# A four-block graph network on one core: gate banks awaited one by one, VectorE's state update moved, expert layers without a barrier between them

## The chip, the cores and the metric

The kernel runs on one core of one Trainium2 chip. Times are device microseconds of that core, median of three runs. TensorE (PE) multiplies matrices into eight PSUM banks, VectorE (DVE) and ScalarE (ACT) work on elements, GpSimd (POOL) does next to nothing here, SyncE (SP) issues most of the transfers (ScalarE can issue some as well). Each engine works through its own list of instructions in order; between engines there are semaphores.

## The reference, cut to what matters

3125 nodes with 128 features, 100000 edges. Four blocks stand one behind the other, each behind a layer norm and with a residual: a gated graph network (GRU cell, four layers), a graph convolution, a relational convolution with eight edge types, and a mixture of eight experts in three layers. The change touches the first and the last.

```python
# gated block, four layers, weights w_ih and w_hh shared
m = x @ weight[l]
agg = segment_sum(m[src], dst)
gi = agg @ w_ih.T + b_ih
gh = x @ w_hh.T + b_hh
r = sigmoid(i_r + h_r)
z = sigmoid(i_z + h_z)
n = tanh(i_n + r * h_n)
x = (1.0 - z) * n + z * x
# expert block, three layers
agg = segment_sum(h[src], dst) / deg
logits = concatenate([h, agg]) @ router_W[l] + router_b[l]
gates = softmax(top_k(logits, 2))
weak = relu(agg @ weak_W[l] + weak_b[l])              # 4 experts
sh = relu(agg @ strong_W1[l] + strong_b1[l])          # 4 experts
strong = sh @ strong_W2[l] + strong_b2[l]
h = h + sigmoid(h @ conf_W[l] + conf_b[l]) * (gates over experts)
```

## The kernel before

**Tiles.** Nodes are cut into 25 tiles of 128 and seven chunks `CH` of 512, 512, 384, 512, 384, 512 and 309 columns, one PSUM bank each. The sum over edges is a product with the dense matrix of edge counts `A` (fp8), which stays in SBUF: per chunk and tile two matmuls (high and low half of the float16 pair), 50 in all.

**Gated block (`block_gru`, `pe_gru`, `act_gru`, `dve_gru`).** Four layers l = 0 to 3, chunks ci = 0 to 6 in each. TensorE: `sum_tile` (L972) sums over edges; `gate_b` (L949) makes the products with the old state into banks BR, BZ and BH; `gate_c` (L959) adds those of the sums and fills BI. ScalarE: sigmoids into `g_r` and `g_z` (L1052, L1054), tanh into `g_n` (L1056). VectorE's `gate_c`: gate sum (L1143, L1146), then after the tanh the state update (L1148, L1151, L1153) into `g_ht`. `finish` of a chunk: TensorE turns the new state to node order in bank 7 (L754), ScalarE writes the high half of `g_h16` or `g_h16b` (L1066) and of `ht16` (L1045), VectorE the low halves (L1167, L1134). Before `gate_b` of chunk n TensorE waits until all banks of chunk n-1 are read out, in three waits together.

Among all this the block does work for a later one, the *mirror steps* (`class Symmetric`): blocks of packed counts are turned by TensorE into bank 6 or 7 in turn (L851), and VectorE adds them to `sym_blocks` (L870). A mirror step of TensorE waits until the step before the last has been added, and in bank 7 also until the last `finish` has freed it (L1167).

The order is written out by hand. In layer 0 the sums of all but two chunks exist before the block begins, and for each chunk ci = 1 to 6 TensorE does `gate_b(ci)`, some sums of layer 1, a mirror step, `gate_c(ci)`, the turning of chunk ci-1, a mirror step. VectorE does a mirror addition, the whole of `gate_c(ci)`, `finish(ci-1)`, a mirror addition. In layers 1 to 3 the gates of chunk ci run among the 25 tiles of the sums of chunk ci+1, by the table `AMONG`: `a` (sums to float16), `b`, `c` (the gates) and `S` (a mirror step) stand before the tile of that number; VectorE and TensorE follow the same table. The last chunk's gates run outside the table.

**Expert block (`block_experts`).** An input stage (layer norm, first product, per-layer scales of the weights) ends in a barrier of all engines. `sp_inputs` stores x to `x_parked`. Then each of three layers runs `dve_layer`, `act_layer`, `pe_layer` and `sp_layer`, and a barrier stands behind each. At a layer's start VectorE finds the largest |h| (L1845 in the first, L1847 in the others), with TensorE's help for the maximum over partitions, and from it a scale (last instruction L1856). ScalarE issues seven transfers for the layer (L2019 to L2025: router and confidence weights and biases, strong bias 1, the two bias rows `m_bias`) and then writes the high halves of `h16` (L2028), VectorE the low halves (L1861), TensorE sums over the edges (L2125). SyncE loads ten weight pieces, each into a room of `wroom`; ScalarE (L2035) and VectorE (L1879) split piece k from room k+1 into a pair in room k, four of them before the first chunk's work, six among it. Then it loads `invd` for each chunk (L1838). L2200 are the weak experts' products, L2164 and L2183 the strong ones'.

## Time and profile before

| | |
|---|---|
| median of three runs (lowest, highest) | 3316.8 us (3315.81, 3319.97) |
| profiled execution, time and span | 3323.0 us, 3320.6 us |
| busy: TensorE, VectorE, ScalarE | 2987.0, 2182.6, 895.6 us |
| mean granted TensorE clock | 0.959 of full |
| gated block | 350 to 822 us |
| expert block, input stage | 1651 to 1696 us |
| expert layers | 1696 to 2228, 2228 to 2757, 2757 to 3287 us |

Times in rows are microseconds from the span's start, where "ns" doesn't stand beside them. In a timeline, the bracket at the end is how long the engine sat idle before the row, and what ended that; rows that repeat directly are merged ("x8"), and the second number is then the time of all. "issue" means that nothing that the profile shows was waited for; ACTq and SPq are transfers issued by ScalarE and SyncE. A granted clock of 1.00 is 2.4 GHz, 0.50 is 1.2 GHz, the only two levels. A buffer's name without its number stands for all of its kind.

### The profile page before, as it was taken

What the parts mean: (1) busy time and instruction counts of PE and PEld (TensorE: products, weight loads), DVE (VectorE), ACT (ScalarE), POOL (GpSimd) and SP (SyncE); (2) the same over time, 40 slices, a digit from 0 to 9 for tenths busy, and PEclk for the clock granted to TensorE, in tenths of its full rate; (3) what the DMA queues carried; (4) which work ended last, traced back from release to release, by engine and by line L of the source; (5) the groups of instructions that cost most, each with busy time, mean ns of one, the idle gap of its engine ahead of it and who ended that gap; (6) DMA issues with size and microseconds to landing.
All of it is one profiled execution on the core that took longest, in us unless ns stands there. A gap on an engine that the chain in (4) does not pass through costs nothing. (4 is left out here: it accounts for less than half of the span.)

```text
span 3320.6 us, 47504 instructions
## 1 busy us (share of the span) xinstructions
PE 2987.0 (90%) x18761; PEld 1792.3 (54%) x18761; DVE 2182.6 (66%) x3982; ACT 895.6 (27%) x1667; POOL 16.7 (1%) x22
## 2 busy tenths in 40 slices
PE   3888789998897999999869999979999997999997
PEld 2666445555443444444535656655666564566565
DVE  7999445555227766766667656676667585666676
ACT  3888322111101000000023222223222233222222
POOL 1000000000000000000000000000000000000000
PEclk8899899999998999999979999999999998999999
DMA  5455246766005555544220000011000002000001
GB/s 123 141 150 157 80 154 220 227 210 201 1 1 164 160 168 165 175 143 135 82 83 3 4 3 4 3 45 40 3 6 5 3 1 83 3 4 3 4 3 41
DMA packets 310958, 265.84 MB, mean 80 GB/s; under 512 B 32767, under 2 KB 289409, under 8 KB 308174
## 3 DMA queue, kind: packets, MB, share of 16 engines
q1 hardware_dynamic: 295694, 256.14, 25.2%
q10 hardware_dynamic: 14624, 5.76, 0.7%
q8 instruction: 153, 2.51, 0.3%
q0 software_dynamic: 416, 0.85, 0.1%
q14 instruction: 71, 0.58, 0.1%
HBM read 172.67 MB, written 90.05 MB: 79 GB/s over the span
## 5 line engine op out<-in xcount | busy, mean ns | idle before, releaser
L1544 PE MATMUL psum<-r_wd,r_h 128*128 128x512 fp8e4 (+1 forms) x2600 | 567.8, 374 | 13.4 <-ACT r_h L226 12.7
L2164 PE MATMUL psum<-m_agg,m_weights 128*128 128x512 f16 (+2 forms) x2016 | 429.5, 366 | 26.9 <-ACT m_agg L2071 26.8
L2125 PE MATMUL psum<-counts,m_h 128*128 128x512 fp8e4 (+2 forms) x2100 | 417.2, 355 | 29.5 <-DVE m_h L1861 29.5
L2183 PE MATMUL psum<-m_weights,x_nodes 128*128 128x256 f16 (+1 forms) x3600 | 413.0, 273 | 17.7 <-DVE m_wtmp L1969 15.6
L1544 PEld LDWEIGHTS psum<-r_wd,r_h 128*128 128x128 f16 x2600 | 240.0, 96 | 306.0 <-issue 16.5
L2183 PEld LDWEIGHTS psum<-m_weights,x_nodes 128*128 128x128 f16 (+1 forms) x3600 | 350.4, 98 | 75.1 <-DVE m_wtmp L1969 22.4
L2125 PEld LDWEIGHTS psum<-counts,m_h 128*128 128x128 f16 x2100 | 206.6, 98 | 226.8 <-issue 37.8
L2164 PEld LDWEIGHTS psum<-m_agg,m_weights 128*128 128x128 f16 x2016 | 198.8, 102 | 240.7 <-issue 56.3
L2083 ACT ACTIVATE m_hT<-m_hT,m_g 128x256 f32<-128x256 f32 x300 | 135.5, 500 | 599.5 <-DVE m_hT L1983 599.5
L2071 ACT ACTIVATE m_agg<-psum,x_nodes 128x512 f32<-128x512 f32 (+2 forms) x336 | 236.4, 716 | 144.4 <-PE psum L2164 116.5
L1983 DVE SCALAR_TENSOR_TENSOR m_hT<-psum,x_nodes,m_bias 128x512 f32<-128x512 f32 (+1 forms) x150 | 112.0, 750 | 169.9 <-PE psum L2200 169.9
L1969 DVE SCALAR_TENSOR_TENSOR m_wtmp<-psum,x_nodes,m_bias 128x256 f32<-128x256 f32 (+1 forms) x300 | 144.8, 483 | 119.9 <-PE psum L2183 116.4
L1960 DVE TENSOR_TENSOR x_nodes<-m_agg,x_nodes 128x512 f16<-128x512 f32 (+2 forms) x336 | 209.7, 624 | 11.6
L2200 PE MATMUL psum<-m_weights,m_agg 128*128 128x512 f16 x900 | 206.5, 379 | 0.0
L676 PE MATMUL psum<-oh_c,oh_s 128*128 128x150 f16 x1566 | 156.2, 237 | 48.5 <-ACT counts L711 31.4
L870 DVE TENSOR_TENSOR sym_blocks<-sym_blocks,psum 128x1024 uint16<-128x1024 uint16 (+1 forms) x169 | 110.4, 664 | 118.6 <-PE psum L851 118.0
L1559 ACT ACTIVATE r_ags<-psum 128x512 f32<-128x512 f32 (+1 forms) x52 | 26.9, 569 | 581.3 <-PE psum L1544 581.3
L676 PEld LDWEIGHTS psum<-oh_c,oh_s 128*128 128x128 f16 x1566 | 112.2, 100 | 111.2 <-issue 68.1
L710 ACT ACTIVATE strip<-psum 128x600 uint16<-128x600 f32 x239 | 162.4, 680 | 34.6 <-PE psum L676 32.8
L972 PE MATMUL psum<-counts,g_h16b 128*128 128x512 fp8e4 (+2 forms) x700 | 159.7, 359 | 2.7 <-DVE g_h16b L1167 2.7
L1972 DVE SCALAR_TENSOR_TENSOR m_h<-m_wtmp,m_g,m_h 128x256 f32<-128x256 f32 (+1 forms) x300 | 145.3, 484 | 10.7
L1276 PE MATMUL psum<-counts,g_h 128*128 128x512 fp8e4 (+2 forms) x700 | 137.2, 355 | 15.9 <-ACT g_h L226 15.2
(290 smaller groups left out, 3389.1 us busy)
## 6 DMA issues: line engine op xcount, KB each, us to landing
r_wd<-packed_sym SPq DMA_DIRECT2D x120, 640.0 KB, 4.2
packed_counts<-strip SPq DMA_DIRECT2D x21, 1800.0 KB, 7.8
sym_blocks<-packed_counts SPq DMA_DIRECT2D x88, 384.0 KB, 4.7
packed_sym<-sym_blocks SPq DMA_DIRECT2D x84, 384.0 KB, 3.3
w_stage<-in_L_gnn_strong_W SPq DMA_DIRECT2D x12, 1024.0 KB, 6.4
m_weights<-in_L_gnn_strong_W SPq DMA_DIRECT2D x21, 512.0 KB, 9.0
x_parked<-x_nodes SPq DMA_DIRECT2D x2, 1600.0 KB, 5.7
x_nodes<-x_parked SPq DMA_DIRECT2D x2, 1600.0 KB, 6.2
```

The source lines that it names most:

```text
L676: m = pe.matmul(psum[:, unit_at(u, w):unit_at(u, w) + UC], oh_s[q][:, k, :, v], oh_c[q][:, k, :, v], start=True, stop=True)
L710: act.activation(typed_home, typed, ACT.Copy, scale=0.5).then_inc(kept_a, 1)
L972: m = pe.matmul(bank[bk][:, 0:cw], h16[l % 2][:, part, i, :], A[:, i, c_:c_ + cw], start=(i == 0 and part == 0), stop=(i == NT - 1 and par ...
L1544: m = pe.matmul(bank[pair[b]][:, 0:2 * cw], h16[:, part, p0 + i, :], f_[:, 2 * b:2 * b + 2, :], start=(p0 + i == 0 and part == 0), stop=(p ...
L1960: vec.tensor_tensor(s_[:, BANK:BANK + cw], wide32, s_[:, 0:cw], ALU.subtract).then_inc(s_split, 1)
L1969: vec.scalar_tensor_tensor(tmp[k % 2][0:r_, :], bank[6 + k % 2][0:r_, 0:H], k_strong[0:r_], bcast[0:r_, ge * H:(ge + 1) * H], ALU.mult, AL ...
L1972: vec.scalar_tensor_tensor(h2[0:r_, i, :], tmp[k % 2][0:r_, :], gates[ci % 2][0:r_, k, ge:ge + 1], h2[0:r_, i, :], ALU.mult, ALU.add).then ...
L2071: act.activation(agg[:, hh % 2, 0:cw], bank[4 + hh % 2][:, 0:cw], ACT.Relu, bias=b1s[:, e * FB + f:e * FB + f + 1], scale=k_hidden).then_i ...
L2125: m = pe.matmul(bank[kb][:, 0:cw], h16[:, part, i, kb * P:(kb + 1) * P], A[:, i, c_:c_ + cw], start=(i == 0 and part == 0), stop=(i == NT ...
L2164: m = pe.matmul(bank[4 + hh % 2][:, 0:cw], w_[:, i, kb, f * P:(f + 1) * P], agg16[:, j, kb, 0:cw], start=(x_ == 0), stop=(x_ == len(todo) ...
L2183: m = pe.matmul(bank[b_][0:r_, 0:H], s_[:, pa[0] * BANK + k * P:pa[0] * BANK + k * P + r_], w_[:, pa[1], f, :], start=(f == 0 and pa == PA ...
L2200: m = pe.matmul(bank[2 + pr % 2][0:r_, :], agg16[:, pa[0], kb, k * P:k * P + r_], w_[:, pa[1], kb, :], start=(y_ == 0), stop=(y_ == len(to ...
```

## The change

Three parts, all in the order of instructions and in waits; the arithmetic is the same.

1. *Gates.* TensorE waits before each group of `gate_b` for its own bank only, for BH until the gate sum's first operation has read it (`g_gated`), and the wait for BI moves to `gate_c`, ahead of its third group.
2. *State.* VectorE's `gate_c` is cut into `gated` (L1142, L1145 afterwards) and `state` (L1152, L1155, L1157). In layer 0 from chunk 1 on `finish(ci-1)` and a mirror addition stand between them; in layers 1 to 3 one mirror addition does, by the letter `d` in the table. Chunk 0 of layer 0 and the last chunk of each layer keep their order.
3. *Experts.* ScalarE issues none of the layer transfers any more. Router and confidence weights and biases of all three layers (now in tiles with room for three) and the bias rows of the first are issued by SyncE in the input stage, behind a clearing by GpSimd that VectorE did before. `sp_layer` loads the pieces of the next layer as soon as the last user of a room in the layer before is through (`room_used`), then the bias rows when the last strong product is added, then `invd`. One barrier stands behind the third layer, none between them.

```diff
@@ -886,7 +886,7 @@
-        AMONG = {1: "S", 3: "a", 4: "S", 6: "S", 7: "b", 9: "S", 11: "c", 13: "S", 16: "S", 19: "S", 22: "S"}
+        AMONG = {1: "S", 3: "a", 4: "S", 6: "S", 7: "b", 9: "S", 11: "c", 13: "Sd", 16: "S", 19: "S", 22: "S"}
...
-                    if n:
-                        pe.wait_ge(g_reset_kept, n)
-                        pe.wait_ge(g_update_kept, n)
-                        pe.wait_ge(g_gated_sum, n)
-                    for g, bk in enumerate((BR, BZ, BH)):
+                    for g, (bk, left) in enumerate(((BR, g_reset_kept), (BZ, g_update_kept), (BH, g_gated))):
+                        if n:
+                            pe.wait_ge(left, n)
...
                     for g, (bk, made_of) in enumerate(((BR, g_reset), (BZ, g_update), (BI, g_input))):
+                        if bk == BI and n:
+                            pe.wait_ge(g_gated_sum, n)
...
-                    gate_c(0, ci)
+                    gated(0, ci)
                     if ci == 0:
+                        state(0, ci)
                         gate_a(0, EARLY + 1)
-                    if ci:
+                    else:
                         finish(0, ci - 1)
                         sym.dve_step()
+                        state(0, ci)
...
+            def load_biases(l):
+                sp.dma_start(bcast[:, 0:NWK * H], bass.AP(m_wb.tensor, m_wb.offset + l * NWK * H, [[0, P], [1, NWK * H]])).then_inc(mbb_in, 16)
+                sp.dma_start(bcast[:, NWK * H:NE * H], bass.AP(m_b2.tensor, m_b2.offset + l * NSG * H, [[0, P], [1, NSG * H]])).then_inc(mbb_in, 16)
...
+                    sp.wait_ge(prio_made, 2)
+                    for l in range(NLAY):
+                        sp.dma_start(rw[:, l, :, 0:NE], m_rw[l].rearrange("(k p) e -> p k e", p=P)).then_inc(mrw_in, 16)
+                        sp.dma_start(rw[:, l, 0:KB, NE:NE + 1], m_cw[l].rearrange("(k p) e -> p k e", p=P), allow_slow_non_contiguous=True).then_inc(mrw_in, 16)
+                        sp.dma_start(rb[:, l, 0:NE], bass.AP(m_rb.tensor, m_rb.offset + l * NE, [[0, P], [1, NE]])).then_inc(mrw_in, 16)
+                        sp.dma_start(rb[:, l, NE:NE + 1], bass.AP(m_cb.tensor, m_cb.offset + l, [[0, P], [1, 1]])).then_inc(mrw_in, 16)
+                        sp.dma_start(b1[:, l], m_b1[l].rearrange("e (k p) -> p (e k)", p=P), allow_slow_non_contiguous=True).then_inc(mrw_in, 16)
+                    load_biases(0)
...
+                def room_used(l, k):
+
+                    if k + 1 == NPC:
+                        sp.wait_ge(s_mixed, NSG * NT * (l + 1))
+                        return
+                    n_, e = ORDER[k + 1]
+                    if n_ == "w1":
+                        sp.wait_ge(s_hidden, hidden_at(l, NCH - 1, e, FB - 1) + 1)
+                    elif n_ == "w2":
+                        sp.wait_ge(s_mixed, mixed_at(l, NCH - 1, e, len(tiles_of(CH[NCH - 1])) - 1) + 1)
+                    else:
+                        sp.wait_ge(k_mixed, NPR * NT * (l + 1))
...
+                        if l:
+                            room_used(l - 1, k)
...
+                    if l:
+                        sp.wait_ge(s_added, NSG * NT * l)
+                        load_biases(l)
...
                 def act_layer(l):
-                    if l == 0:
-                        act.wait_ge(steps.handle, mark["rw_cleared"])
-                    act.dma_start(rw[:, :, 0:NE], m_rw[l].rearrange("(k p) e -> p k e", p=P)).then_inc(mrw_in, 16)
...
-                    act.dma_start(bcast[:, NWK * H:NE * H], bass.AP(m_b2.tensor, m_b2.offset + l * NSG * H, [[0, P], [1, NSG * H]])).then_inc(mbb_in, 16)
                     act.wait_ge(steps.handle, mark["h_scale", l])
...
                     sp_layer(l)
-                    barrier()
+                barrier()
```

*VectorE, gated block, layer 0, chunk 1.* `g_t` is the gate sum's room, `g_h16b` the split state of chunk 0, `sym_blocks` the mirror additions. Before:

```order
L1143 SCALAR_TENSOR_TENSOR g_t_60<-psum,g_sc,g_r_56 128x512
L1146 TENSOR_TENSOR g_t_60<-g_t_60,psum 128x512
L1148 TENSOR_TENSOR g_t_60<-g_ht,g_n_62 128x512
L1151 TENSOR_TENSOR g_t_60<-g_t_60,g_z_58 128x512
L1153 TENSOR_TENSOR g_ht<-g_t_60,g_n_62 128x512
L1167 SCALAR_TENSOR_TENSOR g_h16b<-psum,g_h16b 128x512
L1134 SCALAR_TENSOR_TENSOR g_hn<-g_ht,g_hn 128x512
L870 TENSOR_TENSOR sym_blocks_47<-sym_blocks_47,psum 128x2x512
```

The same place afterwards:

```order
L1142 SCALAR_TENSOR_TENSOR g_t_60<-psum,g_sc,g_r_56 128x512
L1145 TENSOR_TENSOR g_t_60<-g_t_60,psum 128x512
L1171 SCALAR_TENSOR_TENSOR g_h16b<-psum,g_h16b 128x512
L1134 SCALAR_TENSOR_TENSOR g_hn<-g_ht,g_hn 128x512
L870 TENSOR_TENSOR sym_blocks_47<-sym_blocks_47,psum 128x2x512
L1152 TENSOR_TENSOR g_t_60<-g_ht,g_n_62 128x512
L1155 TENSOR_TENSOR g_t_60<-g_t_60,g_z_58 128x512
L1157 TENSOR_TENSOR g_ht<-g_t_60,g_n_62 128x512
```

The three state operations went from ahead of the finish and the mirror addition to behind them.

*VectorE, gated block, layer 1, gates of chunk 1 among the sums of chunk 2.* Before:

```order
L1146 TENSOR_TENSOR g_t_60<-g_t_60,psum 128x512
L1148 TENSOR_TENSOR g_t_60<-g_ht,g_n_62 128x512
L1151 TENSOR_TENSOR g_t_60<-g_t_60,g_z_58 128x512
L1153 TENSOR_TENSOR g_ht<-g_t_60,g_n_62 128x512
L870 TENSOR_TENSOR sym_blocks_49<-sym_blocks_49,psum 128x2x256
L870 TENSOR_TENSOR sym_blocks_46<-sym_blocks_46,psum 128x2x512 x3
```

and afterwards:

```order
L1145 TENSOR_TENSOR g_t_60<-g_t_60,psum 128x512
L870 TENSOR_TENSOR sym_blocks_49<-sym_blocks_49,psum 128x2x256
L1152 TENSOR_TENSOR g_t_60<-g_ht,g_n_62 128x512
L1155 TENSOR_TENSOR g_t_60<-g_t_60,g_z_58 128x512
L1157 TENSOR_TENSOR g_ht<-g_t_60,g_n_62 128x512
L870 TENSOR_TENSOR sym_blocks_46<-sym_blocks_46,psum 128x2x512 x3
```

One mirror addition, that of the step at tile 13, went ahead of the state operations.

*ScalarE, start of the first expert layer* (`m_xT` belongs to the input stage, `m_rw` to `m_bias` are the layer's transfers, `m_h` is `h16`). Before:

```order
L1719 ACTIVATE m_xT_120<-psum 128x128
L2019 DMA m_rw<-in_L_gnn_router_W 128x4x8
L2020 DMA m_rw<-in_L_gnn_conf_W 128x2x1
L2021 DMA m_rb<-in_L_gnn_router_b 128x8
L2022 DMA m_rb<-in_L_gnn_conf_b 128x1
L2023 DMA m_b_127<-in_L_gnn_strong_b 128x16x1
L2024 DMA m_bias<-in_L_gnn_weak_b 128x1024
L2025 DMA m_bias<-in_L_gnn_strong_b 128x1024
L2028 ACTIVATE m_h_125<-m_h,m_sc 128x1280 x5
```

and afterwards:

```order
L1744 ACTIVATE m_xT_121<-psum 128x128
L2059 ACTIVATE m_h_126<-m_h,m_sc 128x1280 x5
L2066 ACTIVATE m_weights<-m_weights,m_wmax_115 128x1024 x4
L2076 ACTIVATE m_hT<-psum 128x512 x2
L2085 ACTIVATE m_agg_105<-m_agg,m_sc 128x1024
```

The seven transfers are gone from this queue, in all three layers; on SyncE's they stand in the input stage, and the bias rows of layers 1 and 2 between the weight pieces and `invd`.

## Rows read from the trace of the kernel before

**Rows 1.** Busy time by stretch: us, PE, PEld, DVE, ACT, POOL, clock, DMA, GB/s.
```profile
389.00:450.80 61.80, 41.86 (x180) 22.56 (x181) 29.11 (x50) 16.47 (x29) 0.00 (x0) 0.80 0.28 91
...
462.00:578.00 116.00, 109.49 (x666) 67.75 (x663) 63.35 (x103) 23.00 (x38) 0.00 (x0) 1.00 0.69 218
```
**Rows 2.** Timeline of TensorE, gated block, layer 0: start, us, what.
```profile
389.04 1.09 PE L851 MATMUL psum<-ident,sym_blocks 128*128 128x128 f32 x4 [4.36 <-DVE g_h16b L1167]
389.92 3.09 PE L949 MATMUL psum<-g_hn,gate_w 128*128 128x384 f16 x9
...
395.33 1.63 PE L959 MATMUL psum<-x_nodes,gate_w 128*128 128x384 f16 x9
396.79 0.60 PE L754 MATMUL psum<-ident,g_ht 128*128 128x128 f32 x4
...
450.81 0.63 PE L851 MATMUL psum<-ident,sym_blocks 128*128 128x128 f32 x4 [3.48 <-DVE g_h16b L1167]
```
**Rows 3.** Timeline of ScalarE, the same layer, chunks 1 and 6.
```profile
385.30 0.81 ACT L1056 ACTIVATE g_n<-g_t,g_b,g_sc 128x512 f32<-128x512 f32 x1 [0.87 <-DVE g_t L1146]
...
386.54 0.57 ACT L1066 ACTIVATE g_h16b<-psum 128x512 f16<-128x512 f32 x1
...
448.94 0.57 ACT L1066 ACTIVATE g_h16b<-psum 128x512 f16<-128x512 f32 x1
```
**Rows 4.** Timeline of VectorE, the same layer, chunks 1 and 6.
```profile
388.21 0.68 DVE L1167 SCALAR_TENSOR_TENSOR g_h16b<-psum,g_h16b 128x512 f16<-128x512 f32 x1
...
449.98 0.68 DVE L1167 SCALAR_TENSOR_TENSOR g_h16b<-psum,g_h16b 128x512 f16<-128x512 f32 x1
```
**Rows 5.** Timeline of TensorE, layer 1, mirror steps at tiles 19 and 22.
```profile
490.24 0.63 PE L851 MATMUL psum<-ident,sym_blocks 128*128 128x128 f32 x4 [1.27 <-DVE sym_blocks L870]
...
491.68 0.60 PE L851 MATMUL psum<-ident,sym_blocks 128*128 128x128 f32 x4
```
**Rows 6.** Timeline of VectorE, the same place.
```profile
487.62 0.69 DVE L1148 TENSOR_TENSOR g_t<-g_ht,g_n 128x512 f32<-128x512 f32 x1 [0.88 <-ACT g_n L1056]
...
489.68 1.01 DVE L870 TENSOR_TENSOR sym_blocks<-sym_blocks,psum 128x512 uint16<-128x512 uint16 x2
```
**Rows 7.** Who waited for whom, 462 to 822 us (us, times, longest); a timeline row.
```profile
PE psum L851 <- DVE sym_blocks L870: 13.8, 13, 1.8
...
570.76 0.63 PE L851 MATMUL psum<-ident,sym_blocks 128*128 128x128 f32 x4 [0.46 <-DVE sym_blocks L870]
```
**Rows 8.** Timeline of ScalarE, start of expert layer 1.
```profile
2227.84 0.45 ACTq L2019 DMA_DIRECT2D m_rw<-in_L_gnn_router_W  x1
...
2230.95 6.27 ACTq L2024 DMA_DIRECT2D m_bias<-in_L_gnn_weak_b  x1
...
2237.78 6.37 ACT L2028 ACTIVATE m_h<-m_h,m_sc 128x1280 f16<-128x1280 f32 x5 [16.66 <-issue]
```
**Rows 9.** Timeline of VectorE, the same place.
```profile
2227.88 0.16 DVE L1847 TENSOR_REDUCE m_sc<-m_hmax 128x1 f32<-128x7 f32 x1 [0.39 <-PEq L104]
...
2229.97 0.15 DVE L1856 TENSOR_SCALAR m_sc<-m_sc 128x1 f32<-128x1 f32 x1
```
**Rows 10.** Timelines of VectorE, ScalarE and SyncE around expert layer 0's start.
```profile
1705.34 0.15 DVE L1856 TENSOR_SCALAR m_sc<-m_sc 128x1 f32<-128x1 f32 x1
...
1707.16 6.37 ACT L2028 ACTIVATE m_h<-m_h,m_sc 128x1280 f16<-128x1280 f32 x5 [14.83 <-issue]
...
1651.02 0.33 SPq L1705 DMA_DIRECT2D x_parked<-x_nodes  x1
1696.20 3.15 SPq L1831 DMA_DIRECT2D m_weights<-in_L_gnn_strong_W  x5
```
**Rows 11.** Timeline of TensorE, first sums of expert layer 1.
```profile
2240.94 23.02 PE L2125 MATMUL psum<-counts,m_h 128*128 128x512 fp8e4 x100 [11.83 <-DVE m_h L1861]
```
**Rows 12.** Timeline of TensorE, a weak product and what follows it.
```profile
2197.12 2.76 PE L2200 MATMUL psum<-m_weights,m_agg 128*128 128x512 f16 x12
2199.72 1.74 PE L2164 MATMUL psum<-m_agg,m_weights 128*128 128x309 f16 x12
```

More of the change, by code:

```diff
@@ L1135, in state_low, with gated @@
                                              ALU.subtract).then_inc(made, 1)
-                def gate_c(l, ci):
-                    n, q = l * NCH + ci, ci % 2
-                    c_, cw = CH[ci]
-                    h_, r_, z_, t_, n_ = ht[:, c_:c_ + cw], rr[q][:, 0:cw], zz[q][:, 0:cw], tt[q][:, 0:cw], nn[q][:, 0:cw]
+                def gated(l, ci):
+                    n, q, cw = l * NCH + ci, ci % 2, CH[ci][1]
+                    r_, t_ = rr[q][:, 0:cw], tt[q][:, 0:cw]
                     vec.wait_ge(g_reset_kept, n + 1)
@@ L1146, in gate_c, with state @@
                     vec.tensor_tensor(t_, t_, bank[BI][:, 0:cw], ALU.add).then_inc(g_gated_sum, 1)
+                def state(l, ci):
+                    n, q = l * NCH + ci, ci % 2
+                    c_, cw = CH[ci]
+                    h_, z_, t_, n_ = ht[:, c_:c_ + cw], zz[q][:, 0:cw], tt[q][:, 0:cw], nn[q][:, 0:cw]
                     vec.wait_ge(g_new, n + 1)
@@ L1183, in among @@
                             if what == "c" and gates_of is not None:
-                                gate_c(l, gates_of)
+                                gated(l, gates_of)
+                            if what == "d" and gates_of is not None:
+                                state(l, gates_of)
                 gate_a(0, EARLY)
@@ L1205, in dve_gru @@
                             gate_a(l, ci)
-                            gate_c(l, ci)
+                            gated(l, ci)
+                            state(l, ci)
                         if 0 < ci < LC:
@@ L1660, in build_program @@
     e_high, e_low = sem("e_high"), sem("e_low")
-    mrw_in, mb1_in, mbb_in, inv_in = sem("mrw_in"), sem("mb1_in"), sem("mbb_in"), sem("inv_in")
+    mrw_in, mbb_in, inv_in = sem("mrw_in"), sem("mbb_in"), sem("inv_in")
     piece_in = [sem(f"piece_in{k}") for k in range(2 * NSG + NWK // 2)]
@@ L1675, in block_experts @@
         NSH = 6
+        MRW_IN = 80 * NLAY
         NPR = NWK * H // BANK
@@ L1679, in block_experts @@
             bcast = sbuf(c, "m_bias", [P, NE * H], F32)
+            b1 = sbuf(c, "m_b1", [P, NLAY, NSG * FB], F32)
             agg = sbuf(c, "m_agg", [P, KB, BANK], F32)
@@ L1682, in block_experts @@
             hT = sbuf(c, "m_hT", [P, KB, BANK], F32)
-            rw = sbuf(c, "m_rw", [P, 2 * KB, NE + 1], F32)
-            rb = sbuf(c, "m_rb", [P, NE + 1], F32)
+            rw = sbuf(c, "m_rw", [P, NLAY, 2 * KB, NE + 1], F32)
+            rb = sbuf(c, "m_rb", [P, NLAY, NE + 1], F32)
             sc = sbuf(c, "m_sc", [P, 4], F32)
@@ L1702, in pool_inputs @@
                               allow_small_or_imprecise_dtypes=True).then_inc(prio_made, 1)
+                    pool.memset(rw[:, :, KB:2 * KB, NE:NE + 1], 0.0).then_inc(prio_made, 1)
                 def sp_inputs():
                     sp.dma_start(xpark, xn[:].rearrange("p i f -> p (i f)")).then_inc(parked, 16)
+                    sp.wait_ge(prio_made, 2)
[6 more added lines that the diff above has]
+                    load_biases(0)
                     sp.wait_ge(parked, 16)
@@ L1771, in block_experts @@
                 wroom = sbuf(c0, "m_weights", [P, NPC, SL], F32)
-                b1 = sbuf(c0, "m_b1", [P, NSG * FB], F32)
                 xroom = xn[:].rearrange("p i f -> p (i f)")
@@ L1842, in dve_layer @@
                     if l == 0:
-                        vec.memset(rw[:, KB:2 * KB, NE:NE + 1], 0.0).then_inc(steps.handle, steps.up())
-                        mark["rw_cleared"] = steps.n
                         vec.tensor_reduce(sc[:, 0:1], h2[:], axis=AX.XY, op=ALU.max, apply_absolute_value=True).then_inc(steps.handle, steps.up())
@@ L1870, in dve_layer @@
                     vec.tensor_tensor(k_weak, sc[:, 2:3], w_inv["ww"], ALU.mult).then_inc(steps.handle, steps.up())
-                    vec.tensor_scalar(b1s[:], b1[:], ks[:, 1:2], None, ALU.mult).then_inc(steps.handle, steps.up())
+                    vec.tensor_scalar(b1s[:], b1[:, l], ks[:, 1:2], None, ALU.mult).then_inc(steps.handle, steps.up())
                     settle()
@@ L1898, in route @@
                         vec.wait_ge(prio_made, 1)
-                        vec.wait_ge(mrw_in, 64 * (l + 1))
+                        vec.wait_ge(mrw_in, MRW_IN)
                         vec.wait_ge(e_routed, n + 1)
@@ L2143, in route @@
                         pe.wait_ge(h_kept, KB * (n + 1))
-                        pe.wait_ge(mrw_in, 64 * (l + 1))
+                        pe.wait_ge(mrw_in, MRW_IN)
                         for i, k in tiles_of(CH[ci]):
```

11 lines of the change are left out of this document (3 added, 8 removed).

## The prediction, made before the changed kernel had run

> **What bounds the kernel now.** I read the busy shares by stretch first, then the timeline of each engine around TensorE's pauses, then the list of who waited for whom. In the stretches that the change touches TensorE is the engine that sets the time: in layer 1 of the gated block (462 to 578 us) it is busy 109.49 of 116 us at a granted clock of 1.00, while VectorE has 63.35 us of work [rows 1]. So a change pays there only where it shortens a pause of TensorE. There are three kinds of such pauses.
>
> - Layer 0 of the gated block, chunks 1 to 6: TensorE is busy only 41.86 of 61.8 us, at a clock of 0.80 [rows 1]. Once per chunk it stops before a mirror step (L851) until VectorE has written `g_h16b` (L1167): 4.36 us in the first of six, 3.48 us in the last [rows 2].
> - Layers 1 to 3: TensorE stops before a mirror step until VectorE has added an earlier one (L870): 13 times, 13.8 us together [rows 7]. An example is 1.27 us at 490.24 [rows 5].
> - The start of each expert layer: TensorE sits idle 11.83 us before its first sums (2240.94) [rows 11], behind ScalarE, which issues seven transfers before its first conversion at 2237.78 [rows 8], though the scale that it needs is there at 2229.97 + 0.15 = 2230.12 [rows 9].
>
> **Gate banks waited for one by one.** In layers 1 to 3 and in layer 0, what frees the banks of chunk n is finished long before TensorE comes to chunk n+1: in layer 0 the pause described above ends behind the whole state update already. The split waits win nothing. Do they cost? Each chunk gets three more waiting matmuls. A row bounds it: twelve matmuls of 512 columns in two groups, each group with waits of its own that are long met, take 2.76 us with the drain, and the next instruction starts 2.60 us after the first, 217 ns each [rows 12]. So 0 us; the bounds are 0 and 27 chunks x 3 x 0.02 = 1.6 us of loss.
>
> **Layer 0: the finish of the chunk before moves ahead of the state update.** Before, VectorE's order is gate sum, (tanh on ScalarE), three state operations, then L1167. Behind the three state operations L1167 starts at 388.21 [rows 4]. Afterwards it follows the gate sum at once, but it also needs ScalarE's half of the same split (L1066), and ScalarE does that behind the tanh: L1056 at 385.30, L1066 at 386.54 for 0.57 us [rows 3]. It ends at 387.11; with 0.1 us for the hand-over L1167 can start at 387.2 instead of 388.21: 1.0 us. So not the whole state update (three operations of 0.69 us each, as in [rows 6]) is saved: ScalarE is late next. The same subtraction in the six chunks gives 1.0, 0.6, 1.2, 0.6, 1.2 and 0.4 us (the last: 449.98 less 448.94 + 0.57 + 0.1 [rows 3, 4]), together **5.0 us**. The state update itself now waits behind the mirror step and is ready about 4 us after TensorE's restart; TensorE asks for it (L754) only behind the next chunk's gates, 396.79 - 389.04 = 7.75 us after the restart [rows 2], so it is covered with 3 to 4 us to spare. Were that cover gone, each us of lateness would count six times.
>
> **Layers 1 to 3: one mirror addition between gate sum and state.** Before, the addition of the step at tile 13 stands behind the state update: VectorE ends the gate sum at 487.62 - 0.88 = 486.74, sits idle for the tanh until 487.62, updates the state, and starts the addition at 489.68 [rows 6]; TensorE was ready for its step at tile 19 at 490.24 - 1.27 = 488.97 [rows 5]. Afterwards the addition (0.42 to 0.69 us) fills the idle 0.88 us, so the pause at tile 19 goes. What is late next is the addition of tile 16's step: the state still ends at about 489.68, this addition at 490.4, and TensorE asks for it one station later, 491.68 - 490.24 = 1.44 us [rows 5] after 488.97, at 490.41. With the hand-over 0.1 us of 1.27 stays. Where the sums have 309 columns instead of 384, each station (tiles 13, 16 and 19) is 0.2 us shorter, so about 0.6 us of such a pause stays. The 13 pauses are three beside 512-column sums, six beside 384, two beside 309, and two like the one of 0.46 us at 570.76 [rows 7], which belong to the last chunk's gates, whose order doesn't change. So 13.8 - 0.9 = 12.9 us can go, and 6 x 0.1 + 2 x 0.6 = 1.8 us stay: **11.1 us** (bounds 0, if the wait only moves to tile 22, and 12.9).
>
> **Expert layers.** The seven transfers leave ScalarE's queue; ScalarE can start its conversion when the scale is there. At the start of layer 1 that is 2237.78 - 2230.12, less 0.07 of hand-over: 7.6 us [rows 8, 9]; layer 2 shows the same rows; at the start of layer 0, where VectorE's reduction of all of `h` covers most of it, 1707.16 - 1705.49 - 0.07 = 1.6 us [rows 10]. Everything behind it (halves of `h16`, sums, weight splits) runs in a chain paced by VectorE, ScalarE and TensorE, not by a transfer, and moves with it. The barrier itself: VectorE's first reduction of the layer (2227.88) comes 0.39 us after its last instruction [rows 9]; without it a hand-over of 0.04 is left: 0.35 us, twice. The weight pieces are now fetched when their rooms come free, so they are earlier than before except for the last two, which follow the last strong product and are needed some 40 us later. On SP's queue the `invd` row of the next layer stands behind these pieces and two bias transfers (one of the kind took ScalarE 6.27 us to issue [rows 8]); from about 2227 that makes 2234, and VectorE needs it only behind four weight splits, some 15 us later: covered. Sum 1.6 + 2 x 7.6 + 2 x 0.35 = 17.5, with the memset taken off VectorE **17.6 us** (bounds 9, half of it, and 19).
>
> Moved onto SP are fifteen small transfers and two biases during the input stage. SP is free there from 1651.35 to the barrier, behind which it issues at 1696.20 [rows 10]: 45 us. Three times the five issues in about 3.0 us, and after each set a stall as long as the longest seen (7 us at most, 6.27 in the row [rows 8]), makes 31 us. Cost 0 (the bound is rival 3).
>
> A rule speaks against this part. The row first: ScalarE spent 2237.78 - 2227.84 = 9.9 us on issuing alone, with 6.27 us for a single transfer [rows 8]. The Trainium skill, "DMA: Bandwidth & Descriptors", section "Issuing engines are not separate DMA queues", says that starting transfers from several engines saves only the sequencer's time, "which is usually small relative to the DMA itself". By it the move would bring next to nothing here and the whole sum 16.9 us instead of 33.7; the row disagrees with "small".
>
> **Sum.** 5.0 + 11.1 + 17.6 = 33.7 us. The profiled execution took 3323.0 us with a span of 3320.6 us, the median of the runs is 3316.8 us, 0.2% less; durations of that size carry over unscaled: 3316.8 - 33.7 = **3283.1 us**.
>
> **Rivals.**
>
> 1. *The clock stays up in layer 0* (13%). After the pause of 4.36 us nine 384-column matmuls take 3.09 us (1.2 GHz); nine of the same width further on take 1.63 us (2.4 GHz) [rows 2]. In layer 1, where the pauses are below 2 us, the clock is 1.00 [rows 1]. The change cuts the six pauses to 3.1 to 3.4 us, between the two. If the clock no longer fell, some 11.5 us more would go (near the bound, 0.20 of 61.8 us = 12.4 us [rows 1]): 3271.6 us. Against it: the pause of 3.48 us still stands in front of a slow stretch. The Trainium skill, "TensorE: Matmul & The Clock Gate", section "HAM oscillation — how this bites in real kernels", has the same mechanism: waits between bursts of matmuls put the clock down and each burst starts slow; it also has shorter waits keep it up, so by that rule this rival would be the forecast. The rows show a fall at the shortest pause of this stretch, so I don't follow it.
> 2. *One half doesn't pay* (15%). In the gated block TensorE's wait may only move: to tile 22 in layers 1 to 3, to ScalarE's half in layer 0. Then 16.1 us shrink to between 5 and 0: 3294 to 3299 us. For it: VectorE's state operations keep their place behind the tanh. Against: the working above leaves 0.1 to 0.6 us per pause. If instead the expert boundary didn't pay: 3301 us (3% of the 15).
> 3. *SP reaches the barrier late* (9%, of it 2% slower than before). Place: the end of the input stage. The stall may belong to the element-wise bias transfer, of which there are now three in one run of issues behind a large store. It decides from 45 us on [rows 10]; every us beyond is a us for all engines. At three stalls of 15 us it would be 9.6 + 45 = 55 us, 10 us late: 3293 us. To end slower than before it would need 45 + 33.7 = 79 us, 23 us per stall: 3317 us and more.
> 4. *No change* (1%): both halves fail.
>
> **Chances.** The forecast (3276 to 3291 us) 62%, and rivals 13, 15, 9 and 1%. About 0.2% (6.6 us) is what a measurement of this kernel can tell from no change. Faster 0.96, same 0.02, slower 0.02. The range goes from 3271 us, just under the first rival, to 3296 us, which takes in rival 3's 3293 and the near half of rival 2.
>
> **What the profile afterwards would show.** Layer 0: TensorE's six pauses at L851 3.1 to 3.4 us, ended by VectorE's split, and that by ScalarE's; if they are still above 4 us, the first step is wrong. Layers 1 to 3: TensorE's waits for the mirror additions fall from 13.8 to 2 to 3 us; if the total stays, with other tiles, rival 2. Expert layers 1 and 2: TensorE's idle before the first sums falls from 11.83 to about 4.2 us, ScalarE issues no transfer, and the sums keep about 23 us. SP's last small issue lies before 1690 us; if VectorE's first reduction of the expert layers comes later than the time shift before it explains, rival 3. The prediction is wrong in its heart if the boundary keeps more than 8 us of idle.

## The result, and the profile after

The changed kernel takes 3278.5 us in the median of four runs (3277.0 to 3285.0), beside 3316.4 us for the kernel before: ratio 0.9887, 95% interval 0.987 to 0.9904, 38.0 us less. On another chip, with four more runs, it was 3282.7 against 3317.2 us, ratio 0.9895 (0.988 to 0.9911), 34.5 us less. The forecast was 33.7 us less, 3283.1 us. The profiled execution after took 3279.3 us with a span of 3277.0 us. The profiled execution before lay 6 us above its median, so the two spans differ by more (43.6 us) than the kernels do: 5.6 us of it lie ahead of the gated block's first gate product, where nothing was changed. Over the thirteen profiled executions that stretch took 365.7 to 371.4 us, whatever the kernel.

Layer 0 of the gated block, in the busy times by stretch (us, PE, PEld, DVE, ACT, POOL, clock, DMA, GB/s): first the kernel before, from the first gate product to the end of the sixth pause, then the changed kernel in the execution of record, then in the one on the other chip.

```profile
371.34:450.81 79.47, 55.20 (x260) 30.25 (x259) 38.70 (x65) 24.14 (x41) 0.00 (x0) 0.83 0.25 78
```
```profile
365.74:438.30 72.56, 53.19 (x259) 29.33 (x259) 37.35 (x62) 23.70 (x40) 0.00 (x0) 0.86 0.27 85
```
```profile
370.90:437.13 66.23, 46.85 (x260) 27.27 (x259) 37.26 (x62) 23.73 (x40) 0.00 (x0) 0.95 0.30 94
```

The stretch less TensorE's busy time is the six pauses: 24.27, 19.37 and 19.38 us. The pauses shrank by 4.9 us in both. The rest is clock, and it is not the same in two executions of one program: 53.19 and 46.85 us of busy time for the same products. TensorE's timeline after, first, second and sixth pause, answers to [rows 2]; the last two rows are the first pause in the execution on the other chip, where the same products ran at full clock (1.63 instead of 2.40 us):

```profile
382.46 0.63 PE L851 MATMUL psum<-ident,sym_blocks 128*128 128x128 f32 x4 [3.38 <-DVE g_h16b L1171]
382.92 2.40 PE L947 MATMUL psum<-g_hn,gate_w 128*128 128x384 f16 x9
...
393.51 0.41 PE L851 MATMUL psum<-ident,sym_blocks 128*128 128x128 f32 x2 [3.22 <-DVE g_h16b L1171]
...
438.30 1.09 PE L851 MATMUL psum<-ident,sym_blocks 128*128 128x128 f32 x4 [3.13 <-DVE g_h16b L1171]
...
387.61 0.63 PE L851 MATMUL psum<-ident,sym_blocks 128*128 128x128 f32 x4 [3.38 <-DVE g_h16b L1171]
388.08 1.63 PE L947 MATMUL psum<-g_hn,gate_w 128*128 128x384 f16 x9
```

The second pause, in ScalarE's and VectorE's timelines (answers to [rows 3, 4]): VectorE's split begins 0.11 us after ScalarE's half ends at 392.57, as forecast, with the state update behind it.

```profile
392.00 0.57 ACT L1066 ACTIVATE g_h16b<-psum 128x512 f16<-128x512 f32 x1
...
392.68 0.69 DVE L1171 SCALAR_TENSOR_TENSOR g_h16b<-psum,g_h16b 128x512 f16<-128x512 f32 x1 [1.84 <-ACT g_h16b L1066]
```

Layers 1 to 3, who waited for whom from 462 to 822 us (us, times, longest), and the step at tile 19 of layer 1, whose pause was 1.27 us [rows 5, 7]. The waits that are left make 2.0 us, where 2 to 3 us were forecast; the step at tile 19 begins 0.08 us after the row ahead of it ends:

```profile
PE psum L851 <- issue: 1.1, 2, 0.5
PE psum L851 <- DVE sym_blocks L870: 0.9, 2, 0.5
...
476.03 1.14 PE L972 MATMUL psum<-counts,g_h16b 128*128 128x384 fp8e4 x6
477.25 0.63 PE L851 MATMUL psum<-ident,sym_blocks 128*128 128x128 f32 x4
```

Start of expert layer 1 (VectorE, ScalarE, TensorE), against [rows 8, 9, 11]: the conversion begins 0.03 us after the scale is there, and TensorE's idle fell from 11.83 to 4.21 us. The first sums took 23.58 us after 23.02, at a granted clock of 0.92 after 0.94. SP's last two rows are the last small issue of the input stage and the next one behind the barrier, against [rows 10]: 28 us of SP were left over.

```profile
2202.66 0.15 DVE L1896 TENSOR_SCALAR m_sc<-m_sc 128x1 f32<-128x1 f32 x1
...
2202.84 6.37 ACT L2059 ACTIVATE m_h<-m_h,m_sc 128x1280 f16<-128x1280 f32 x5 [8.69 <-DVE m_sc L1896]
...
2206.01 23.58 PE L2156 MATMUL psum<-counts,m_h 128*128 128x512 fp8e4 x100 [4.21 <-DVE m_h L1901]
...
1643.75 0.43 SPq L1707 DMA_DIRECT2D m_bias<-in_L_gnn_strong_b  x1
1672.11 2.76 SPq L1870 DMA_DIRECT2D m_weights<-in_L_gnn_strong_W  x5
```

### The profile page after: what moved, and what is told of

It is laid out like the page before. It is cut to its first block and busy times, and to the rows that moved or that the text cites. A ratio compares the mean times of both kernels' runs of the same rounds, so it can differ in the third digit from the quotient of the medians.

```text
span 3277.0 us, 47453 instructions
## 1 busy us (share of the span) xinstructions
PE 2972.4 (91%) x18761; PEld 1787.6 (55%) x18761; DVE 2182.7 (67%) x3981; ACT 895.8 (27%) x1667; POOL 16.7 (1%) x23
## 5 line engine op out<-in xcount | busy, mean ns | idle before, releaser
L2195 PE MATMUL psum<-m_agg,m_weights 128*128 128x512 f16 (+2 forms) x2016 | 421.8, 362 | 33.5 <-ACT m_agg L2102 33.5
## 6 DMA issues: line engine op xcount, KB each, us to landing
sym_blocks<-packed_counts SPq DMA_DIRECT2D x88, 384.0 KB, 4.5
packed_sym<-sym_blocks SPq DMA_DIRECT2D x84, 384.0 KB, 3.3
```

The costliest lines, as they stand in the source:

```text
L2195: m = pe.matmul(bank[4 + hh % 2][:, 0:cw], w_[:, i, kb, f * P:(f + 1) * P], agg16[:, j, kb, 0:cw], start=(x_ == 0), stop=(x_ == len(todo) ...
```

## The experiments

All were timed in turn with the kernel before on the same chip, in three groups (the first four, the next three, the last four). The medians of before were 3318.2, 3316.3 and 3317.2 us. Parts of a few us are read from intervals between two fixed points of the trace. The layer 0 column is the stretch shown above, from its first gate product to the end of its sixth pause. "Layers 1 to 3" is from the end of layer 0's sixth pause to the first sums of the block behind; "one expert layer" is from the first sums of layer 1 to those of layer 2.

| kernel | ratio to before (95%) | layer 0, us | its clock | layers 1 to 3 | one expert layer |
|---|---|---|---|---|---|
| before | 1 | 79.5 | 0.83 | 383.6 | 529.5 |
| layer 0 order | 0.9984 (0.9975 to 0.9993) | 73.5 | 0.84 | 383.6 | 529.3 |
| layers 1 to 3 order | 0.9963 (0.995 to 0.9977) | 76.1 | 0.89 | 370.3 | 529.0 |
| expert part | 0.9946 (0.9932 to 0.9959) | 79.4 | 0.83 | 383.7 | 521.7 |
| banks | 0.9999 (0.999 to 1.0008) | 79.5 | 0.83 | 384.0 | 528.6 |
| all (changed kernel) | 0.9887 (0.987 to 0.9904) | 72.6 | 0.86 | 370.3 | 520.2 |

### The four parts alone

**Layer 0 order.** In VectorE's layer 0 loop only:

```diff
-                    gate_c(0, ci)
+                    gated(0, ci)
                     if ci == 0:
+                        state(0, ci)
                         gate_a(0, EARLY + 1)
-                    if ci:
+                    else:
                         finish(0, ci - 1)
                         sym.dve_step()
+                        state(0, ci)
```

> The kernel before with one edit: in layer 0 of the gated block VectorE does the finish of the chunk before and the mirror addition ahead of the state update. Forecast of the step: six pauses of TensorE fall to 3.1 to 3.4 us, 5.0 us less. The trace of the changed kernel gives 20.2 us for the whole gated block where 16.1 was forecast; if the rest of 4.1 us is clock that layer 0 regained, this run gives 7 to 9 us and its granted clock from 389 to 446 us is above that of before; if the rest lies in layers 1 to 3, it gives 5 us. If ScalarE's half is what TensorE waits for and the order of VectorE is without weight, 0.

Measured: 0.9984, 5.3 us less (2.3 to 8.3). The pauses are 3.38, 3.22, 3.14, 3.22, 3.27 and 3.12 us, together 19.35 after 24.27: 4.9 us, as forecast. In this execution the clock gave back 1.1 us beside it, so the larger number expected from a regained clock did not show here. It was the slowest of this kernel's eleven executions (3306.3 to 3318.0 us), so it doesn't speak for the others.

**Layers 1 to 3 order.** `AMONG` has "Sd" at tile 13, and only what that needs.

```diff
-        AMONG = {1: "S", 3: "a", 4: "S", 6: "S", 7: "b", 9: "S", 11: "c", 13: "S", 16: "S", 19: "S", 22: "S"}
+        AMONG = {1: "S", 3: "a", 4: "S", 6: "S", 7: "b", 9: "S", 11: "c", 13: "Sd", 16: "S", 19: "S", 22: "S"}
```

> The kernel before with one edit: in layers 1 to 3 the state update stands behind the mirror addition of tile 13. Forecast of the step: 11.1 us less, 1.8 of 13.8 us of the pauses stay. If the station behind it is not late at all, as the trace of the changed kernel suggests (only pauses of about 0.5 us left), 12 to 12.9 us. If the wait moves to tile 22 instead (the rival), 0.

Measured: 0.9963, 12.3 us less (7.6 to 16.6), and 383.6 to 370.3 us in the trace: 13.3 us, more than either of the expected numbers. Comparing the starts of the gate products in both traces, a pause of 0.47 us gave 0.67 us, one of 1.27 gave 1.19, one of 1.32 gave 1.45 and one of 1.82 gave 1.26; five chunks without a listed pause gave another 0.1 us each. Why a pause can give more than its bracket can be seen in the timeline of the kernel before:

```profile
486.42 1.14 PE L972 MATMUL psum<-counts,g_h16b 128*128 128x384 fp8e4 x6
487.39 0.60 PE L851 MATMUL psum<-ident,sym_blocks 128*128 128x128 f32 x4
487.83 1.14 PE L972 MATMUL psum<-counts,g_h16b 128*128 128x384 fp8e4 x6
```

A row of six matmuls with 384 columns lasts 1.14 us, and without a pause the next row starts 0.97 us after its start; the one at 487.83 is followed by the pause of 1.27 us, and the next row [rows 5] starts 1.14 + 1.27 us after it. So a pause costs 0.17 us more than its bracket. Layer 0 was not touched in this kernel, and its stretch came out 3.3 us shorter all the same, at a clock of 0.89.

**Expert part.** The kernel before with everything that the change does from `block_experts` on, and nothing in the gated block.

```diff
-                    act.dma_start(rw[:, :, 0:NE], m_rw[l].rearrange("(k p) e -> p k e", p=P)).then_inc(mrw_in, 16)
...
-                    barrier()
+                barrier()
```

> The kernel before with the expert part alone (no transfer issued by ScalarE, no barrier between the layers, weight pieces fetched room by room). Forecast of the step: 17.6 us less. The traces of before and after differ by 19.5 us behind the input stage; if that belongs to the edit and not to the one execution, 19 to 20 us. If the gain needed the earlier start of the gated block, less than 17.

Measured: 0.9946, 17.9 us less (13.6 to 22.6): the forecast, and it needs nothing of the gated block. One expert layer took 521.7 us after 529.5 to 528.6 in four kernels with the old boundary, 7.4 us on average; the changed kernel's own was 520.2.

**Banks.** In `pe_gru` each bank's first matmul waits for what frees that bank, and nothing else is changed.

```diff
-                    if n:
-                        pe.wait_ge(g_reset_kept, n)
-                        pe.wait_ge(g_update_kept, n)
-                        pe.wait_ge(g_gated_sum, n)
-                    for g, bk in enumerate((BR, BZ, BH)):
+                    for g, (bk, left) in enumerate(((BR, g_reset_kept), (BZ, g_update_kept), (BH, g_gated))):
+                        if n:
+                            pe.wait_ge(left, n)
...
+                        if bk == BI and n:
+                            pe.wait_ge(g_gated_sum, n)
```

> The kernel before with one edit: TensorE waits for each gate bank by itself. Forecast: 0 us, bounds 0 and 1.6 us of loss. The rival, that the split wait lets the first matmuls of a chunk's gates start earlier: it would show as a shorter idle time ahead of the gates' first matmul (L946 and thereabouts) and 1 us or more of gain.

Measured: 0.9999 (0.999 to 1.0008). The nine products of a chunk take 2.11 and 1.63 us as before, layer 0 79.47 us as before, and layers 1 to 3 came out 0.4 us longer. No gain, and no price that could be told from nothing.

The four parts together give 5.3 + 12.3 + 17.9 + 0.3 = 35.8 us, and the changed kernel 38.0 and 34.5 us. These parts come from the ratios; the medians as they stand differ by 5.7, 14.8, 19.2 and 1.6 us, 41.2 us together. Either way they add up within the intervals, and no part covers another by an amount that could be seen.

### The expert boundary: barrier, or issues?

**Barrier kept.** The changed kernel, with the barrier back in the loop over the layers.

```diff
                     sp_layer(l)
-                barrier()
+                    barrier()
```

> The changed kernel with one edit: the barrier at the end of every expert layer is back; ScalarE still issues nothing. Since every weight piece waits for the barrier again, two terms could show: the barrier itself, 0.35 us twice, so 0.7 us slower than the changed kernel; and the weight pieces, which land later. If the pieces are not waited for (as forecast), 0.7 us in all, and 37 us faster than before; if they are, each layer start is some us longer and ScalarE's wait ahead of its weight splits names a DMA.

Measured: 0.9913 (0.99 to 0.9927), 29 us less than before. VectorE's first reduction comes 0.39 us after its last instruction, where the changed kernel has 0.04 us (2200.57 behind 2199.58 + 0.95): 0.35 us at a boundary, as forecast. TensorE's idle ahead of the first sums is 4.21 us as without the barrier. The median is 8.5 us above the changed kernel's, and the traces don't lay that on the barrier. The profiled execution is 4.1 us longer, 2.4 us of it between the first sums of layers 0 and 1 (523.9 after 521.4 us); but in the changed kernel's execution on the other chip, without a barrier, that stretch took 523.6 us and the next one 521.2, here 523.9 and 521.4. What does part the medians stays open; the two intervals touch.

**ScalarE issues again, no barrier.**

```diff
                 def act_layer(l):
+                    if l:
+                        act.wait_ge(s_added, NSG * NT * l)
+                    act.dma_start(rw[:, l, :, 0:NE], m_rw[l].rearrange("(k p) e -> p k e", p=P)).then_inc(mrw_in, 16)
...
```

> The changed kernel with one edit: the seven small transfers of each layer stand at the start of the layer on ScalarE's queue again; the barriers stay away. If the 9.9 us of issuing are the price (forecast), it is 1.6 + 2 x 7.6 = 16.8 us slower than the changed kernel, and TensorE's idle ahead of the first sums of layers 1 and 2 is back near 11.8 us. If the barrier was the price and ScalarE without it issues during the tail of the layer before, at most 2 us slower. Since the biases wait for VectorE's last addition, which comes 1 us before the barrier's end, I expect the first: 16 us.

Measured: 0.991 (0.9897 to 0.9924), 5 to 8 us slower than the changed kernel, not 16. **This expectation was wrong.** ScalarE's timeline at the start of layer 1:

```profile
2204.08 0.39 ACTq L2045 DMA_DIRECT2D m_rw<-in_L_gnn_router_W  x1
...
2206.06 0.46 ACTq L2049 DMA_DIRECT2D m_b<-in_L_gnn_strong_b  x1
2206.54 3.20 ACTq L2050 DMA_DIRECT2D m_bias<-in_L_gnn_weak_b  x1
2209.77 0.46 ACTq L2051 DMA_DIRECT2D m_bias<-in_L_gnn_strong_b  x1
2210.28 6.37 ACT L2054 ACTIVATE m_h<-m_h,m_sc 128x1280 f16<-128x1280 f32 x5 [11.61 <-issue]
```

The seven issues take 6.2 us and not the 9.9 of [rows 8], because the long one is 3.20 us and not 6.27; TensorE's idle is 7.13 us. Without the barrier SP has issued the weight pieces of the layer before ScalarE comes to its own. Over the three layers the idle is 5.25, 7.13 and 7.06 us after 4.2 each, 6.8 us more, as much as the slowdown. So the two halves of the expert part overlap: issues away, barrier kept gives 7.6 us of idle; barrier away, issues kept gives 11.83 - 7.13 = 4.7 us; both give 7.6 us.

**Which transfer makes the issue long?** In the changed kernel SP issues the same transfers in the input stage, and the long rows there are not the biases' own: the longest each time is whatever stands directly behind `m_b` (its source is read element by element, 128 partitions of 16). The first of the three sets, behind the store of x, has three more issues of 1.0 to 1.3 us, which the others don't have.

```profile
1631.49 0.47 SPq L1729 DMA_DIRECT2D m_b<-in_L_gnn_strong_b  x1
1632.00 3.97 SPq L1725 DMA_DIRECT2D m_rw<-in_L_gnn_router_W  x1
...
1637.55 0.43 SPq L1729 DMA_DIRECT2D m_b<-in_L_gnn_strong_b  x1
1638.03 1.81 SPq L1725 DMA_DIRECT2D m_rw<-in_L_gnn_router_W  x1
...
1641.41 0.43 SPq L1729 DMA_DIRECT2D m_b<-in_L_gnn_strong_b  x1
1641.89 1.81 SPq L1706 DMA_DIRECT2D m_bias<-in_L_gnn_weak_b  x1
```

SP's burst of weight pieces is the other suspect. The kernel of the last experiment has both cases: at layer 0, behind the input stage's barrier, SP issues the pieces at the same time, and the issue behind `m_b` takes 6.60 us; at layers 1 and 2, without them, it takes 3.20 and 3.12 us.

```profile
1677.21 6.60 ACTq L2050 DMA_DIRECT2D m_bias<-in_L_gnn_weak_b  x1
...
1677.19 4.67 SPq L1855 DMA_DIRECT2D m_weights<-in_L_gnn_weak_W  x4
```

Two kernels test the order, with the same edit in the kernel of the last experiment and in the kernel before: this one transfer is issued last of the seven. The changed kernel ran again beside them.

```diff
-                    act.dma_start(b1[:], m_b1[l].rearrange("e (k p) -> p (e k)", p=P), allow_slow_non_contiguous=True).then_inc(mb1_in, 16)
                     act.dma_start(bcast[:, 0:NWK * H], bass.AP(m_wb.tensor, m_wb.offset + l * NWK * H, [[0, P], [1, NWK * H]])).then_inc(mbb_in, 16)
                     act.dma_start(bcast[:, NWK * H:NE * H], bass.AP(m_b2.tensor, m_b2.offset + l * NSG * H, [[0, P], [1, NSG * H]])).then_inc(mbb_in, 16)
+                    act.dma_start(b1[:], m_b1[l].rearrange("e (k p) -> p (e k)", p=P), allow_slow_non_contiguous=True).then_inc(mb1_in, 16)
```

> The changed kernel once more, on the same chip as the next three. In the run with the barrier kept the trace is 4.1 us longer than that of the changed kernel, but the medians, taken on different chips, are 8.5 us apart. If that is the chip, this run's ratio to before is about 0.989 to 0.990; if the barrier really costs 8 us, it stays at 0.9887. Stretches in which nothing differs should again scatter by 1 to 3 us.

> The kernel with ScalarE's seven transfers and no barrier, with one edit: the element-by-element transfer of the strong biases (m_b1) is issued last, behind the two broadcast transfers, instead of ahead of them. If the long issue (3.20 us) is long because it stands behind that transfer, no issue of the seven is above 1 us, they end about when the scale is there, and TensorE's idle ahead of the first sums of layers 1 and 2 falls from 7.1 to 4.2 to 4.8 us: some 6 us faster than with the old order. If the broadcast transfer itself is long to issue, or the sixth in a row is, it stays long, and idle stays near 7 us.

> The kernel before with the same edit alone: the strong biases' transfer last of the seven. If the 6.27 us belong to the transfer ahead of it, the seven issues shrink from 9.9 to about 4 us, TensorE's idle at layers 1 and 2 falls from 11.83 to about 6 us, and the kernel is 11 to 13 us faster than before with two moved lines. If the burst of weight transfers that SP issues at the same moment makes the issue long, about half of it stays: 6 us faster. If the broadcast is long by itself, 0.

Measured on one chip: the changed kernel 0.9895 (0.988 to 0.9911), so by the ratios 6.0 us and not 8.6 part it from the kernel with the barrier kept, and whether the 2.7 us are the chip or scatter two measurements can't tell. ScalarE's issues without barrier, `m_b` last: 0.9896 (0.9881 to 0.9911), as fast as the changed kernel. The kernel before with the one transfer moved: 0.9959 (0.9946 to 0.9973), **13.5 us less**. ScalarE's timeline of the last one, start of layer 1, against [rows 8], and TensorE's first sums:

```profile
2220.32 0.56 ACTq L2023 DMA_DIRECT2D m_bias<-in_L_gnn_weak_b  x1
2220.91 0.53 ACTq L2024 DMA_DIRECT2D m_bias<-in_L_gnn_strong_b  x1
2221.47 1.37 ACTq L2025 DMA_DIRECT2D m_b<-in_L_gnn_strong_b  x1
2222.89 6.37 ACT L2028 ACTIVATE m_h<-m_h,m_sc 128x1280 f16<-128x1280 f32 x5 [12.03 <-issue]
...
2226.05 23.38 PE L2125 MATMUL psum<-counts,m_h 128*128 128x512 fp8e4 x100 [7.19 <-DVE m_h L1861]
```

The broadcast's issue fell from 6.27 to 0.56 us, and the idle from 11.83 to 7.19 us, from 11.87 to 6.27 and, at layer 0, from 5.85 to 4.21: 4.6 + 5.6 + 1.6 = 11.9 us. That carries the 13.5 us within its interval; that execution also had the clock in layer 0 at 0.89. With `m_b` last and no barrier the seven issues of layer 1 take 3.5 us, none above 0.55 us, and idle is 4.44 us. So the long issue belonged to the transfer ahead of it, and it was about twice as long where SP's burst ran beside it. Part of the stall can still turn up elsewhere: in layer 2 of the same kernel `m_b` itself took 2.09 us and idle was 6.02 us, and where ScalarE had `m_b` last beside the burst, SP's own issues of the four weak pieces took 6.07 to 7.71 us instead of 3.53 to 5.25.

### What is late next in layer 0

```diff
-                def gate_c(l, ci):
+                def gate_c(l, ci, turned=None):
...
+                    if turned is not None:
+                        kept_high(l, turned)
...
+                    if turned is not None:
+                        turned_high(l, turned)
                     act.wait_ge(g_gated_sum, n + 1)
...
-                    gate_c(0, ci)
+                    gate_c(0, ci, turned=ci - 1 if ci else None)
...
-                    if ci:
-                        finish(0, ci - 1)
```

`turned_high` writes the high half of the turned state, now ahead of the tanh; `kept_high` writes the scaled state (L1045), now ahead of the sigmoids.

> The changed kernel with one edit: in layer 0 ScalarE makes the high half of the turned state ahead of the tanh, and the scaled state ahead of the sigmoids. If ScalarE's half is what is late next, TensorE's six pauses fall from 3.1 to 3.4 us to about 1.7 us: 9 us less than the changed kernel. If the clock of TensorE then no longer falls in this stretch, up to 11 us more: 20 us less. If something else is late next (the tanh now waits), 0 to 3 us.

Measured: 0.9833 (0.982 to 0.9847), 3260.3 us. The pauses fell to 1.57, 1.57, 1.33, 1.58, 1.45 and 1.57 us, and the clock no longer falls:

```profile
368.09:421.13 53.04, 43.96 (x260) 26.16 (x259) 37.08 (x62) 24.64 (x40) 0.00 (x0) 1.00 0.37 117
...
390.73 0.41 PE L851 MATMUL psum<-ident,sym_blocks 128*128 128x128 f32 x2 [1.57 <-DVE g_h16b L1179]
390.97 2.11 PE L947 MATMUL psum<-g_hn,gate_w 128*128 128x512 f16 x9
```

Beside the changed kernel's 72.56 us the stretch is 19.5 us shorter: 10.3 us of pauses (19.37 less 9.08) and 9.2 us of clock (53.19 less 43.96 of busy time). Beside the changed kernel's other execution (66.23 us) it is 13.2 us shorter, with the same 10.3 us of pauses. The median is 18 us below the changed kernel's, 22 us below that on the other chip. So ScalarE's half was what TensorE waited for, and the full price of the clock in this stretch is 55.20 - 43.96 = 11.2 us, taken from two kernels with the same products.

One more edit puts the last two finishes of a layer 4 and 2 tiles earlier in layers 2 and 3:

```diff
-                        if l > 0 and ci == 0 and i == tiles_of(CH[LC - 1])[0][0]:
+                        if l > 0 and ci == 0 and i == tiles_of(CH[LC - 1])[0][0] - (4 if l > 1 else 0):
                             finish(l - 1, LC - 1)
-                        if l > 0 and ci == 0 and i == tiles_of(CH[LC])[0][0]:
+                        if l > 0 and ci == 0 and i == tiles_of(CH[LC])[0][0] - (2 if l > 1 else 0):
                             finish(l - 1, LC)
```

> The kernel in which ScalarE turns first, with one more edit: at the start of layers 2 and 3 the last two finishes of the layer before stand 4 and 2 tiles earlier in the order of TensorE and VectorE. There TensorE waits 1.49 and 1.33 us twice for the split of the turned state. If tiles and mirror steps in between cover that wait, up to 5 us less than the kernel it starts from; if the wait moves to the next mirror step that uses the same bank, 0 to 1 us.

Measured: 0.9826 (0.9813 to 0.984), 3258.5 us, 58.7 us less than before. Timing alone doesn't part it from 0.9833. The trace does: from the first gate product to the end of the block it is 3.5 us shorter, and the four waits are two of 0.7 and two of 0.5 us instead of 1.49 and 1.33 twice.

## Why the prediction held, and where its terms were off

- **Banks, 0 us.** Right: 0.9999.
- **Layer 0, 5.0 us.** Right in size and cause: 4.9 us of pauses, with ScalarE's half late next. Each pause lies in the forecast 3.1 to 3.4 us. The cover for the state update held.
- **The clock in layer 0 (rival 1, 11.5 us).** Its size was right, 11.2 us, but "the clock stays up" or "it falls" was the wrong pair. At pauses of 3.1 to 3.4 us part of it comes back, and how much differs between executions: over the six executions with the new order, TensorE's busy time in the stretch was 54.1, 53.2, 50.1, 50.1, 50.1 and 46.9 us (clock 0.84 to 0.95), 50.7 on average, and with the old order 55.2 three times and 51.9 twice (0.83 and 0.89), 53.9 on average. The two sets overlap, so the 3 us between the averages are an indication and no more. So the step that failed is "the rows show a fall at the shortest pause of this stretch, so I don't follow it": one execution was read as a rule, and a fall at 3.48 us says nothing certain of pauses of 3.1 to 3.4. The forecast should have carried a term of about 3 us with a bound of 8 (55.2 less 46.9). The Trainium skill, "TensorE: Matmul & The Clock Gate", section "HAM oscillation — how this bites in real kernels", describes short waits that leave the clock up; the 1.3 to 1.6 us pauses at a clock of 1.00 agree with it, and the pauses of 3.1 to 3.4 us agree in part only: in the execution of record a slow row follows each of the six, on the other chip only the second, fourth and sixth. By that section the clock would have stayed up there too; the measured clocks decide.
- **Layers 1 to 3, 11.1 us.** The mechanism was right, the term too small: 13.3 us. The brackets undercount a pause by 0.17 us, and of the four pauses of 1.32 us nothing stayed: they gave 1.45 us each. Of the two of 1.27 us 0.1 us stayed, as forecast, and the pauses at the 309-column sums kept 0.55 us each, where 0.6 was said. The stated upper bound of 12.9 us was passed because it was a sum of brackets, and for the five places that gave 0.1 us each.
- **Experts, 17.6 us.** Right: 17.9 us alone; idle 4.21 us where about 4.2 was said. What was too simple is the reason, that the seven transfers hold ScalarE for 9.9 us: 4.6 and 5.6 us of the 7.6 at the two boundaries, and all 1.6 at layer 0, belong to the place of one transfer among them. Rival 3 had named that transfer as the possible owner of the stall, but it entered neither the sum nor its reason. The total held because the change removes the issues altogether. The Trainium skill, "DMA: Bandwidth & Descriptors", section "Issuing engines are not separate DMA queues", calls the sequencer's time for starting a transfer usually small beside the transfer itself. The runs agree for most issues (0.4 to 0.6 us, where these transfers land 2.2 us or more after their issue) and disagree for one behind the element-by-element transfer (1.81 to 6.27 us); the 17.9 us that the part gave side with the row.
- **SP late at the barrier (rival 3).** Didn't happen: three stalls of 3.97, 1.81 and 1.81 us instead of 7 each, and 28 us to spare. The 7 us had been read where SP's burst ran beside the issue.
- **One half doesn't pay (rival 2).** Fell: each half paid alone.
- **The sum.** Forecast 33.7; the parts alone 35.8; measured 38.0 and 34.5. The 2.2 us of layers 1 to 3 are the part that the forecast lacked in every execution. The rest is no more than what stretches do from one execution to the next that are the same in both kernels or in which only the clock differs: layer 0 of the changed kernel 66.2 to 72.6 us, the stretch ahead of the gated block 365.7 to 371.4 us. That 34.5 us came within 1 us of the forecast is therefore partly luck.

## What to carry to other kernels

When an engine's wait is cut, look at once for the half that is late next: here two operations moved on ScalarE gave another 18 us, since the shorter pauses also kept TensorE's clock up. When an engine spends microseconds on issuing, find out which issue is long and what stands directly ahead of it before moving all of them to another queue; the order alone was worth 13.5 us. And check a stretch with pauses in several executions before its clock is put into a sum.

## What the runs showed of the hardware

- Most issues take 0.4 to 0.6 us, but one directly behind `m_b`, which is read element by element (8 KB), took 1.8 to 4.1 us on SyncE's queue in the input stage, 3.1 and 3.2 us on ScalarE's, and 5.3 to 7.5 us on ScalarE's beside SyncE's burst of weight pieces. Behind the confidence weights, also read element by element but only 1 KB, it took 0.5 us, and 1.3 us once per execution right behind the store of x. Why, the runs don't show.
- The same program ran layer 0 with 46.85 and with 53.19 us of TensorE busy time. The pauses were the same to 0.01 us in sum. It is the largest difference that a stretch showed between two executions of the same program here.
- Rows of matmuls that follow without a pause overlap in the timeline (a 1.14 us row, the next 0.97 us after its start). A pause of TensorE there costs 0.17 us more than the idle time shown for it.
- With pauses of 1.33 to 1.58 us the granted clock of layer 0 was 1.00 in both executions, with pauses of 3.12 to 3.38 us 0.84 to 0.95 in six, and with pauses of 3.48 to 4.48 us 0.83 or 0.89 in five.
